# Second attention of a two-layer transformer kernel: transpositions between the two turns of the scores, and two products of the identity's bits per tile

## The reference

```python
OFFSETS = sorted(set(range(0, 33)) | {48, 64, 96, 128, 192})      # 38 offsets, 16 heads of 8
q, k, v = split(x @ Wqkv.T + bqkv)
scores = einsum('bhnd,bhond->bhno', q, K_all) * scale             # K_all: the key o tokens back
scores = where(n_idx < offs, -inf, scores + pos_bias)
alpha = softmax(scores)
out = einsum('bhno,bhond->bhnd', alpha, V_all)
return flat(out) * sigmoid(x @ Wgate.T + bgate) @ Wout.T + bout
```

## Time and profile before

| | |
|---|---|
| median of 3 runs | 1504.06 us (1499.51 to 1507.79) |
| the profiled execution | 1515.03 us, span 1513.2 us |
| PE busy | 1247.5 us, 82% of the span |
| DVE busy | 1114.4 us, 74% |
| ACT busy | 815.7 us, 54% |
| POOL busy | 685.6 us, 45% |
| mean granted clock of TensorE | 0.893 |

### The profile page before, as it was taken

One profiled execution on the slowest core, in us unless ns is written; L12 is line 12 of the kernel. 1 busy time (PEld: TensorE's weight loads), 2 busy tenths in 40 slices (PEclk: granted clock), 3 DMA queues, 4 the chain that ended last, 5 costly groups with the idle time before them and its releaser, 6 DMA issues.

```text
span 1513.2 us, 40070 instructions
## 1 busy us (share of the span) xinstructions
PE 1247.5 (82%) x14676; PEld 892.7 (59%) x14676; DVE 1114.4 (74%) x3616; ACT 815.7 (54%) x1971; POOL 685.6 (45%) x1042
## 2 busy tenths in 40 slices
PE   4499889988899988999988899589989998647780
PEld 2255545555455554555556899467777777547660
DVE  5588687886878868888665665558788878755666
ACT  1155555555555555555555455178787657326663
POOL 3023241233432334323223654466666768674664
PEclk9699999999999999999999899777887757668995
DMA  5656727556275572755741311022111112222335
GB/s 120 108 96 91 115 29 117 87 92 107 30 121 81 91 115 28 119 81 91 119 181 35 102 47 30 25 69 63 46 45 44 35 34 76 99 68 81 89 85 173
DMA packets 73892, 123.37 MB, mean 82 GB/s; under 512 B 17534, under 2 KB 46083, under 8 KB 72800
## 3 DMA queue, kind: packets, MB, share of 16 engines
q1 hardware_dynamic: 63896, 104.97, 36.6%
q0 software_dynamic: 7616, 13.59, 2.8%
q10 hardware_dynamic: 2184, 2.25, 0.8%
HBM read 30.40 MB, written 17.60 MB: 32 GB/s over the span
## 4 chain that ended last, share of the span: by engine, by line
PE 43%; DVE 28%; POOL 9%; ACT 8%; issue 6%; DMA 3%; ACTq 1%; DVEq 1%; SPq 0%; POOLq 0%
DVE first L843 7%; PE A L640 6%; DVE S L846 4%; PE S L1099 4%; PE S L611 4%; PE S L622 4%; PE S L1659 3%; DVE tA L822 3%; POOL xq L1468 2%; PE A L1670 2%; PE A L1106 2%; DMA Qp<-mT 2%; DVE tB L823 2%; PE S L1645 2%; PE S L1676 2%
## 5 line engine op out<-in xcount | busy, mean ns | idle before, releaser
L727 ACT ACTIVATE P<-S 128x512 f32<-128x512 f32 (+3 forms) x768 | 330.6, 491 | 285.6 <-PE S L622 283.3
L622 PE MATMUL S<-Qp,Kp 121*128 121x512 f32 (+3 forms) x768 | 258.2, 394 | 39.1 <-DMA Qp<-mT 11.8
L907 POOL TENSOR_SCALAR_AFFINE_SELECT P<-P 128x256 f32<-128x256 f32 x256 | 112.6, 443 | 373.8 <-ACT P L727 373.1
L846 DVE CUSTOM_DVE_ANT_0 S<-S,later 128x512 f32<-128x512 f32 (+3 forms) x512 | 238.9, 514 | 53.7 <-PE S L611 52.4
L611 PE MATMUL S<-Kp,Qp 120*128 120x512 f32 (+3 forms) x768 | 243.4, 389 | 30.7 <-DMA Kp<-big 16.3
L622 PEld LDWEIGHTS S<-Qp,Kp 121*128 121x128 f32 x768 | 137.4, 190 | 123.9 <-DVE first L843 24.6
L843 DVE TENSOR_REDUCE first<-S 128x1 f32<-128x512 f32 x256 | 164.3, 682 | 55.0 <-PE S L611 54.5
L611 PEld LDWEIGHTS S<-Kp,Qp 120*128 120x128 f32 x768 | 132.9, 194 | 112.5 <-issue 49.7
L640 PE MATMUL A<-P,V 128*9 128x256 f32 (+1 forms) x2816 | 174.5, 343 | 5.4 <-POOL P L907 4.6
L640 PEld LDWEIGHTS A<-P,V 128*9 128x9 f32 x2816 | 63.9, 90 | 70.9 <-issue 29.8
L1896 POOL TENSOR_TENSOR prod<-mid,kT 128x128 f32<-128x128 f32 x160 | 68.0, 459 | 72.1 <-ACT mid L1727 45.4
(11 more groups left out here) (358 smaller groups left out, 2585.7 us busy)
## 6 DMA issues: line engine op xcount, KB each, us to landing
Qp<-big SPq DMA_DIRECT2D x63, 256.0 KB
Kp<-big SPq DMA_DIRECT2D x62, 256.0 KB
Qp<-big SPq DMA_DIRECT2D x63, 128.0 KB
Kp<-big SPq DMA_DIRECT2D x62, 128.0 KB
xq<-xq SPq DMA_DIRECT2D x71, 72.0 KB
yb<-yq SPq DMA_DIRECT2D x8, 528.0 KB, 7.2
big<-in_w SPq DMA_DIRECT2D x4, 1024.0 KB, 9.9
big<-vt SPq DMA_DIRECT2D x32, 128.0 KB
```

What stands on the lines that cost most here:

```text
L622: te.matmul(S[s][:, 512 * h + c:512 * h + 512], K[0:121, h, 128 * kb:128 * kb + 128], Q[0:121, h, 512 * qh + c:512 * qh + 512], start=True ...
L727: se.activation(k.P[(w.n - 1) % NP0][:, h, c:512], S[s][:, 512 * h + c:512 * h + 512], ACT.Exp, scale=SCALE0).then_inc(p.done("st").h, 1)
L846: ins = ve.tensor_tensor_reduce(out=of, in0=of, in1=k.later[:, 512 - n:512], scale=1.0, scalar=-3e38, op0=ALU.add, op1=ALU.max, accum_out= ...
L907: ge.affine_select(P[:, :, c:c + 128], P[:, :, c:c + 128], [[0, 2], [1, 128]], ALU.is_ge, 0.0, base=0, channel_multiplier=-1).then_inc(p.s ...
```

## The change

Two things change, in the list of work and in PE's part of it.

First, the scores of a tile become two items. `sc0` is the first turn, put into the list just ahead of `pt`; `sc` is the second turn, where `sc` was. So the eight transpositions of tile t-3 stand between the two turns on PE. All waits of the scores move ahead with `sc0`: keys, masked queries, and the reading of the score bank by DVE (`done("sc")` of the tile before). `sc` keeps the wait for `pe_sc0`.

Second, `keep_awake` adds a product whose result is not used: the identity's 128x128 f32 words read as bf16, weights 128x128 (the first 128 of 256 halves), moving operand 512 columns (the 256 halves twice). It is called ahead of the first turn, into the score bank, after `sc0`'s waits, and ahead of the far logits, into bank L, after the wait for that bank and before the wait for POOL's products. Scores and logits then write over the results.

```diff
@@ Attn1.order, step t
             if t >= 4:
                 self.slot["av", t - 4] = o.add("av", t - 4, ring="V").slot
+            if t < NT:
+                o.add("sc0", t)
             if 0 <= t - 3 < NT:
                 o.add("pt", t - 3, ring="P")
@@
+def keep_awake(te, p, bank):
+
+    bits = p.ident[:].bitcast(BF16)
+    te.matmul(bank, bits[:, 0:128], bits[:, None, :].broadcast_to([128, 2, 256]), start=True, stop=True)
@@ attn1_tensor
-        elif w.kind == "sc":
+        elif w.kind in ("sc0", "sc"):
             t = w.at[0]
-            c, i = t // 4, t % 4
-            pe.wait_ge(p.done("k1"), 2 * c + 2)
-            pe.wait_ge(p.sem("a_qm"), 2 * c + 2)
-            for turn in range(2):
-                for j in range(4):
...
-                if turn == 0:
-                    pe.wait_ge(p.sem("pe_sc0"), 2 * w.n)
-            ins.then_inc(p.made("sc").h, 1)
+            c, i, turn = t // 4, t % 4, int(w.kind == "sc")
+            if turn == 0:
+                pe.wait_ge(p.done("k1"), 2 * c + 2)
+                pe.wait_ge(p.sem("a_qm"), 2 * c + 2)
+                if t:
+                    pe.wait_ge(p.done("sc"), t)
+                keep_awake(te, p, C[:, 0:512])
+            else:
+                pe.wait_ge(p.sem("pe_sc0"), 2 * w.n)
+            for j in range(4):
...
+            if turn:
+                ins.then_inc(p.made("sc").h, 1)
         elif w.kind == "lo":
             t = w.at[0]
+            keep_awake(te, p, L[:])
             pe.wait_ge(p.sem("g_prod"), w.n)
```

More of the change, by code:

```diff
@@ L1647, in attn1_tensor @@
             ins.then_inc(p.made("vw").h, 1)
-        elif w.kind == "sc":
+        elif w.kind in ("sc0", "sc"):
             t = w.at[0]
-            c, i = t // 4, t % 4
-            pe.wait_ge(p.done("k1"), 2 * c + 2)
-            pe.wait_ge(p.sem("a_qm"), 2 * c + 2)
-            for turn in range(2):
-                for j in range(4):
[L1655 to L1662, removed]
-                if turn == 0:
-                    pe.wait_ge(p.sem("pe_sc0"), 2 * w.n)
-            ins.then_inc(p.made("sc").h, 1)
+            c, i, turn = t // 4, t % 4, int(w.kind == "sc")
[8 more added lines that the diff above has]
+            for j in range(4):
+                for g in (turn, 2 + turn):
+                    rows, h = slice(32 * g, 32 * g + 32), 4 * g + j
+                    for q in range(4):
+                        at = WAY - 32 + 128 * i + 32 * q
+                        ins = te.matmul(C[32 * q:32 * q + 32, 64 * h:64 * h + 64], k.Qm[c % 2][rows, j, 128 * i + 32 * q:128 * i + 32 * q + 32],
+                                        k.kT[c % 2][rows, at:at + 64], start=True, stop=True, tile_position=(32 * g, 32 * q))
+                    if turn == 0 and j == 3:
+                        ins.then_inc(p.sem("pe_sc0").h, 1)
+            if turn:
+                ins.then_inc(p.made("sc").h, 1)
         elif w.kind == "lo":
             t = w.at[0]
+            keep_awake(te, p, L[:])
             pe.wait_ge(p.sem("g_prod"), w.n)
```

## The result

The change made the kernel **slower: 1529.79 us median** (four executions, 1525.60 to 1532.27) against 1501.78 for the kernel before in the same comparison (four, 1497.72 to 1507.79). The ratio is 1.0162, with a 95% interval of 1.0122 to 1.0202: 28 us of the medians. I had forecast 1499, with a range to 1517.

What follows compares the result with a forecast made beforehand. PE, busy at a low clock, was taken to bound the second attention's late chunks. Late chunks -8.6 us, early +3.6, first and last zero: -5.0 from the median 1504.06 gives 1499, with a range of 1480 to 1517.

Steps and rivals of the forecast that it cites:

- the clock's allowance: Second attention, chunks 1 to 6: most clock falls should go, leaving 1.5 us a chunk for work still at 1.2 GHz.
- the baseline of the gain: Whole kernel: the 5.0 us gain, worked out from one profiled execution, was subtracted from the median of 1504.06 us.
- What bounds the kernel: Second attention: PE, busy 89 to 94% of each chunk at a clock of 0.66 to 0.81, with DVE next in line.
- The product, 0.25 us: PE's line, two a tile: 0.25 us each at full clock, 0.45 at 1.2 GHz; 16 us for 64 if nothing hid it.
- The pause that is filled: PE before the second turn: transpositions fill 0.27 us a tile, 8.6 us in 32 places, giving up to 9 us back.
- The loops of ACT: ACT's steps from copy to copy, in a loop with PE: 39.5 us a late chunk, 34.6 an early one, at full clock.
- Rival B: Second attention: clock stays at 0.75 or under, PE remains the bound and pays for the products; 17 us slower, 1521; chance 0.20.
- Rival A: Second attention: clock at 0.95 or over, later transpositions absorbed; some 22 us faster, 1482; chance 0.27.
- Rival C: Late chunks: transpositions don't count for the clock, only products raise it, half the gain goes; -0.7 us, 1503; chance 0.08.
- the rule under it: TensorE's clock: the skill says transposing doesn't engage the full clock or count as PE-busy the same way; sum then rival C's.

Runs made afterwards that it cites:

- before's first profile: The kernel before, unedited, in the profile read for the prediction: 1515.03 us.
- the second profile: The kernel before, run once more with no edit to get another profile: 1502.81 us.

## Why the prediction was wrong

I forecast -5 us and measured +28. The step that failed is the clock's allowance, 9 us for six chunks, of which 21.8 were measured; the baseline of the gain came on top. By the steps of the prediction:

- **What bounds the kernel** held as far as it went: PE in the late chunks, at 1.2 GHz. But ACT waited 44.4 us for PE's transpositions already, and I took the late chunks' time to fall with PE's clock.
- **The product, 0.25 us**, was right. By starts it takes 0.32 us ahead of the scores and 0.22 ahead of the far logits at 2.4 GHz (1133.83 to 1134.15, 1136.75 to 1136.97), 0.54 and 0.39 at 1.2 GHz. Two a tile make 32 x 0.54 = 17 us of the line, where 16 were forecast. The figure that the Trainium skill gives (TensorE: Matmul & The Clock Gate, Back-to-back issue gap; 0.216 us worked out from it) agrees with the second place, not with the first. The same section calls it the gap of a single product in isolation; a product put behind another one took 0.20 to 0.23 us here (0.52 less 0.32, 0.45 less 0.22), which agrees too.
- **The pause that is filled** was right: 0.7 us left of 8.6. That it would be worth 9 us was not tested by itself; the far logits in the same place gave 8 to 10, with a higher clock as well.
- **The loops of ACT** were right: of eight steps five within 0.12 us, two more within 0.32 and 0.62; 34.98 us for chunk 3 against 34.6 forecast, 41.5 for chunk 4 against 39.5, of which 1.9 is the last step. ACT's idle time ahead of the first tile's copy, forecast as some 2 us, was 2.29 us at the start of chunks 3 and 4 and 3.71 and 4.05 where chunks 2 and 5 begin. That nothing would move ahead of the second attention held within 2.2 us: its first key product starts at 981.97 where before's first profile has 979.77.
- **"The clock", an allowance of 1.5 us a chunk**, is the term that failed. The six chunks are over the loops at the full clock (34.6 and 39.5) by 3.2, 7.9, 0.4, 0.2, 8.2 and 1.9 us, 21.8 together where I had 9.0: 13 us. Early chunks took 115.3 us for the 108.3 forecast, late ones 128.8 for 123.0. Two chunks out of six ran some 60% of their time at 1.2 GHz (an estimate from their clocks of 0.69 and 0.71). There a loop has its product, turn and transpositions at 3.54 us for 2.13, and the value windows at 1.98 (1063.30) for 1.15. I had priced one stretch of scores and transpositions at the low clock in each chunk. In two chunks the low clock lasted much longer, and every operation of the loop paid for it, not only that stretch. That the products would buy time by the clock failed as well: they raised it and the time stayed (with the moved transpositions 1529.79 us with them and 1532.56 without, in two jobs).
- **The baseline** is the second failed step. I took the late chunks' gain from one profile of the kernel before, that had a low clock (0.893) and ran 11 us over the median, and then subtracted that gain from the median. By the second profile the six chunks had taken 11 us less to begin with. From -5, 13 for the clock and 11 for the baseline make +19. Ahead of chunk 1 the change's profile is 4.5 us later than that second profile (1018.9 against 1014.4), behind chunk 6 it takes 0.6 less: that gives +22.7, the difference of the two spans. Why the first 4.5 came about isn't settled; 2.2 of them stand against before's first profile too. The other 5 us lie between profiles and medians: the change's profile is 4 us under its own median, the second one of before (1502.81) 1 us over the 1501.78 that the change was compared with.
- **Rival B** (1521) had the sign and came nearest. Its mechanism is refuted: it had the products cost PE's line, at a clock of 0.75 or under. Over the six chunks the clock was 0.83, and without products the order is just as slow. **Rival A** had part of the clock right (0.95, 0.96 in two chunks), and the time didn't follow: what ACT waits for lies in the loop. I had that argument written against it.
- **Rival C** and the rule under it (the Trainium skill, the same page, Part 4: transpositions don't count for the clock) stay open. Transpositions between the turns without products left the clock at 0.77 and 0.71 over the two groups of chunks, not above the kernel before (0.80 and 0.71, 0.88 and 0.72); products without the transpositions raised it. That fits the rule. But the order also brought ACT's and PE's standstills, and no run separates the two. The return of the clock in the earlier trace rows, which I took to disagree with the rule, came behind 64 value products as well as transpositions, so it can't decide.

What is shown: the order costs it all; it costs by what waits behind ACT's copy (with the copy behind the exponentials the cost is gone); the products change the time by nothing that these runs can tell, in each of four comparisons (in the old order once and twice, in the change's, with the far logits between the turns; the one in the change's order is between two jobs of four executions each). What isn't shown: where the low clock of chunks 2 and 5 comes from. A standstill of 3.96 us stands ahead of the fall in chunk 2, one of only 0.83 ahead of that in chunk 5, and the kernel before had chunks at 0.63 and 0.66 without the change. So why the clock's term came out at 21.8 us stays open.

## What to carry to other kernels

Before an operation is moved later on a busy engine, look at who waits for it and what stands behind that wait: here 1.1 us of transpositions, moved behind a wait and a turn of 0.8 us in each tile, cost 28 us, since ACT had its copy and its exponentials behind them, and the same gap filled with work that is read late went with a gain of 8 to 10. A rise in the clock is no gain by itself: set it against the loop that ends last. And if one execution of a program differs from the next by more than the effect in question, take the gain and the baseline from the same execution, or from several.

## What was unexpected of the hardware

- Products put in to raise the clock did raise it, from 0.72 (the second profile of before) to 0.84 and 0.87 in chunks 4 to 6 with 64 and 128 of them, and over whole executions from 0.899 to 0.906 and from 0.898 to 0.915. The time stayed within 0.5%: ratios of 1.0010 and 1.0001.
- The clock was at 0.88 there with the far logits between the turns and not one product more, and at 0.84 in the second profile of that kernel. The kernel before had 0.71 and 0.72. Why a mere reordering does that I can't say from these runs.
- The same program gets a mean clock of 0.886 to 0.907 from execution to execution on a single core (19 executions), and its time, which goes with it, spreads over 20 us, 1.4%.
- A product of 512 columns takes 0.39 us in its record at the full clock, and the next instruction starts 0.22 us after it where 16-column products follow, and 0.32 where 32x32 blocks follow (1136.75 and 1133.83). The two places write different banks too, so what follows need not be the reason.
